# Turning the row maxima of an attention kernel on VectorE in 32 by 32 blocks, and its early maxima in pairs

## The reference, cut to what matters

```python
x = _layernorm(builder_state, g1, beta1)         # 4096 x 512
base_n = _layernorm(base_state, g1, beta1)       # 3202 x 512
q, k, v = (heads(q_in, Wq, bq), heads(kv_in, Wk, bk), heads(kv_in, Wv, bv))   # 8 heads of 64
scores = jnp.einsum('bhqd,bhkd->bhqk', q, k) * (1.0 / np.sqrt(HD))
attn = jax.nn.softmax(scores, axis=-1)
out = jnp.einsum('bhqk,bhkd->bhqd', attn, v)
x = residual + out @ W_o.T + b_o
...
```

## Time and profile before

| | us |
|---|---|
| median of 3 runs | 2254.17 (2253.38 to 2255.58) |
| the profiled execution | 2255.61 |
| its span | 2253.8 |
| PE busy | 2216.3 (98% of the span) |
| DVE busy | 1713.4 (76%) |
| POOL busy | 1584.2 (70%) |
| ACT busy | 1092.4 (48%) |
| weight loads of PE | 1279.2, beside its matmuls |

### The profile page before, as it was taken

How to read it: one execution, slowest core, us unless ns; L and a number is a source line. 1 busy time by engine, 2 the same in 40 slices (tenths; PEclk the granted TensorE clock), 3 DMA queues, 4 the chain that set the end, 5 groups by cost and what they waited for, 6 DMA issues and landing times.

```text
span 2253.8 us, 36015 instructions
## 1 busy us (share of the span) xinstructions
PE 2216.3 (98%) x14120; PEld 1279.2 (57%) x14120; DVE 1713.4 (76%) x2087; ACT 1092.4 (48%) x1418; POOL 1584.2 (70%) x1038
## 2 busy tenths in 40 slices
PE   8999999999999999999999999999999999999997
PEld 8998865555555555555555555555555555445774
DVE  7866546888888888888888888888888888763776
ACT  5654334444454444444544544444445444453454
POOL 1200027888888888888888888888888888889332
PEclk9999999999999999999999999999999999999999
DMA  7750226777777777777777777777777777787844
GB/s 273 233 162 10 75 85 139 156 157 160 156 159 160 159 170 168 171 170 167 168 161 160 167 170 171 171 171 164 163 163 165 167 166 166 160 182 159 265 149 150
DMA packets 170091, 365.45 MB, mean 162 GB/s; under 512 B 28537, under 2 KB 75001, under 8 KB 169410
## 3 DMA queue, kind: packets, MB, share of 16 engines
q0 software_dynamic: 59904, 218.13, 47.4%
q1 hardware_dynamic: 110018, 145.02, 20.3%
HBM read 95.82 MB, written 49.04 MB: 64 GB/s over the span
## 4 chain that ended last, share of the span: by engine, by line
PE 94%; DMA 1%; ACT 1%; DVE 1%; issue 1%; POOL 1%; SPq 0%; DVEq 0%; ACTq 0%; POOLq 0%
PE ps L1478 34%; PE ps L1343 11%; PE ps L1455 8%; PE ps L1457 8%; PE ps L1459 8%; PE ps L1447 5%; PE ps L1306 4%; PE ps L1314 3%; PE ps L1324 3%; PE ps L1545 3%; PE ps L1278 1%; DMA acca<-pt 1%; PE ps L1348 1%; PE ps L1488 1%; PE ps L1608 1%
## 5 line engine op out<-in xcount | busy, mean ns | idle before, releaser
L799 ACT ACTIVATE pt<-ps 128x1024 f32<-128x1024 f32 x800 | 777.6, 1021 | 891.8 <-PE ps L1459 882.0
L1005 DVE TENSOR_REDUCE mx_part<-ps 128x2 f32<-128x1024 f32 x768 | 938.1, 1221 | 339.5 <-PE ps L1343 339.5
L605 POOL TENSOR_TENSOR accp<-accp,pt 128x1024 f32<-128x1024 f32 x416 | 1032.9, 2483 | 210.0 <-ACT pt L799 204.7
L1478 PE MATMUL ps<-pt,v 128*64 128x512 f32 x3328 | 805.6, 605 | 0.0
L1094 DVE TENSOR_TENSOR ps<-ps,shb 128x1024 f32<-128x1024 f32 x403 | 493.2, 1224 | 46.7 <-PE ps L1459 46.7
L1478 PEld LDWEIGHTS ps<-pt,v 128*64 128x64 f32 x3328 | 201.8, 136 | 345.2 <-issue 339.0
L1343 PE MATMUL ps<-kk,qh 64*128 64x512 f32 x1520 | 344.4, 448 | 1.6 <-DVE mx_part L1005 1.6
L1343 PEld LDWEIGHTS ps<-kk,qh 64*128 64x128 f32 x1520 | 141.6, 183 | 340.9 <-DVE mx_part L1005 250.0
L1455 PE MATMUL ps<-qh,kk 64*128 64x512 f32 x1664 | 328.9, 390 | 2.7 <-ACT pt L799 2.7
L1457 PE MATMUL ps<-qh,kk 64*128 64x512 f32 x1664 | 329.3, 390 | 0.0
L1459 PE MATMUL ps<-ql,kk 64*128 64x512 f32 x1664 | 328.5, 389 | 0.0
(11 more groups left out here) (165 smaller groups left out, 1779.7 us busy)
## 6 DMA issues: line engine op xcount, KB each, us to landing
acca<-pt POOLq DMA_DIRECT2D x224, 512.0 KB, 4.9
accb<-pt POOLq DMA_DIRECT2D x160, 512.0 KB, 4.8
q_scratch<-kk SPq DMA_DIRECT2D x32, 512.0 KB, 4.3
acca<-accp POOLq DMA_DIRECT2D x32, 512.0 KB, 4.6
o_scratch<-ost SPq DMA_DIRECT2D x32, 512.0 KB, 3.1
og<-o_scratch SPq DMA_DIRECT2D x32, 512.0 KB, 6.2
shb<-m_scratch SPq DMA_DIRECT2D x31, 512.0 KB, 4.6
xs<-x SPq DMA_DIRECT2D x16, 512.0 KB, 6.5
```

Of the source, the lines that this page charges most:

```text
L605: nc.gpsimd.tensor_tensor(acc[:, :], acc[:, :], pt[n % PT_SLOTS][:, :], ALU.add).then_inc(added_p, 1)
L799: nc.scalar.activation(pt[n % PT_SLOTS][:, :], src, ACT.Exp, scale=SCALE).then_inc(exped, 1)
L1005: nc.vector.tensor_reduce(mx_part[w % 2][:, m % QT, :, m // QT], ps[:, b:b + 2, :], AX_X, ALU.max)\
L1478: ins = mm(ps[HD * h:HD * (h + 1), 6, :], v[:, t, f:f + HD], pt[n % PT_SLOTS][:, h * QB:(h + 1) * QB], start=(t == 0), stop=(t == NT - 1))
```

## The change

**Turning.** PE's `turn_max` and ACT's `shift` are gone. `mx_row` is now a tile of 32 columns, of which 8 are used. DVE turns it with one instruction behind the reduction, in four blocks of 32 by 32, into `mx_turn`: the 8 values of partitions 0 to 31 then lie in rows 0 to 7, those of partitions 32 to 63 in rows 32 to 39, and so on. SP sends them with four stores of 8 rows of 32 numbers, where it was one store of 8 rows of 128. The sign is changed no more: the row of ones is now one of -1, and DVE subtracts where it added. DVE waits for its own reduction before it turns, and for the stores of the unit before.

**Pairs.** In groups 2 to 11 of the context stage the second early maximum follows the first at once on PE. It goes to banks 0 and 1, which are free between `turn` of the next group and that of the one after it; the latter now waits for that maximum to be taken. DVE takes the first maximum behind the first low part of k, and the second behind the second one.

```diff
-        mx_row = at("mx_row", [P, 2, QT], RR + 11776)
+        mx_row = at("mx_row", [P, 32], RR + 11840, F32R)
+        mx_turn = at("mx_turn", [P, 32], RR + 11872, F32R)
...
 def max_bank(w, m):
+    if w == 0 and m % 2 == 1 and m < 2 * (C_G - 3):
+        return 0
     return 5 if (w, m) in EARLY else 4
...
             def send_shift(w):
-                sp.wait_ge(shift_ready, w + 1)
+                sp.wait_ge(max_ready, w + 1)
...
-                sp.dma_start(m_scratch[w % 2].rearrange("h (q k) -> (h q) k", k=P), shift_row[:, :].bitcast(F32)).then_inc(sh_stored, 16)
+                by_tile = m_scratch[w % 2].rearrange("h (q k) -> (h q) k", k=P)
+                for i in range(4):
+                    sp.dma_start(by_tile[:, 32 * i:32 * (i + 1)], mx_turn[32 * i:32 * i + 2 * QT, :].bitcast(F32)).then_inc(sh_stored, 16)
...
-            def shift(w):
-                act.wait_ge(max_turned, w + 1)
-                wait(act, sh_stored, 16 * w)
-                nc.scalar.activation(shift_row[:, :], ps[0:2 * QT, turn_bank(w), 0:P], ACT.Copy, scale=-1.0)\
-                    .then_inc(shift_ready, 1)
...
             def row_max(w):
...
-                nc.vector.tensor_reduce(mx_row[:, :, :].rearrange("p h q -> p q h"), mx_part[w % 2][:, :, :, :], AX_X, ALU.max)\
-                    .then_inc(max_ready, 1)
+                nc.vector.tensor_reduce(mx_row[:, 0:2 * QT].rearrange("p (h q) -> p q h", h=2), mx_part[w % 2][:, :, :, :], AX_X, ALU.max)\
+                    .then_inc(row_ready, 1)
+                dve.wait_ge(row_ready, w + 1)
+                wait(dve, sh_stored, 64 * w)
+                nc.vector.transpose(mx_turn[:, :].bitcast(F32), mx_row[:, :].bitcast(F32)).then_inc(max_ready, 1)
...
                     if n == 12:
                         dve.wait_ge(parts_loaded, 32)
+                        nc.vector.memset(mx_row[:, :].bitcast(F32), 0.0).then_inc(row_cleared, 1)
...
             def turn(n):
                 pe.wait_ge(normed, n + 1)
                 wait(pe, n_ready, 2 * n)
+                if second_max(n - 2 - X_G):
+                    pe.wait_ge(max_taken, nth_max(*second_max(n - 2 - X_G)) + 1)
...
             def maxima(w, m):
-                wait(pe, max_taken, nth_max(w, m))
+                if max_bank(w, m) == 0:
+                    wait(pe, max_taken, nth_max(w, m) - 1)
+                    pe.wait_ge(n_ready, 2 * (X_G + m // 2 + 2 + 2))
+                else:
+                    wait(pe, max_taken, nth_max(w, m))
...
-            def turn_max(w):
-
-                pe.wait_ge(max_ready, w + 1)
-                wait(pe, den_taken, w - 1)
-                if w == 0:
-                    pe.wait_ge(n_ready, 2 * NG)
-                nc.tensor.transpose(ps[0:2 * QT, turn_bank(w), 0:P], mx_row[:, :, :].rearrange("p h q -> p (h q)"), ident[:, :])\
-                    .then_inc(max_turned, 1)
...
-                        early_maxima(early[:1])
+                        early_maxima(early[:2])
                         project_v(n, 1)
-                        early_maxima(early[1:2])
```

More of the change, by code:

```diff
@@ L55, in maxima_of @@
     return [(i // NM, i % NM) for i in range(first, min(first + 2, NM * UNITS))]
-TURN_STEP = NJ - M_LEAD
 PAIR_ORDER = [2, 3, 0, 1]
@@ L133, in unit, with second_max @@
     return w % BLOCKS, PAIR_ORDER[w // BLOCKS]
+def second_max(g):
+    return (0, 2 * (g - 2) + 1) if 2 <= g < C_G - 1 else None
 def max_bank(w, m):
+    if w == 0 and m % 2 == 1 and m < 2 * (C_G - 3):
+        return 0
     return 5 if (w, m) in EARLY else 4
-def turn_bank(w):
-    return 7 if w else 0
 def k_slot(w):
@@ L236, in build @@
         ost = at("ost", [P, 2, QB], RR + 10240, F32R)
-        mx_row = at("mx_row", [P, 2, QT], RR + 11776)
+        mx_row = at("mx_row", [P, 32], RR + 11840, F32R)
+        mx_turn = at("mx_turn", [P, 32], RR + 11872, F32R)
         mx_part = [at("mx_part0", [P, QT, 2, 7], RR + 12032), at("mx_part1", [P, QT, 2, 7], RR + 11784)]
-        shift_row = at("shift_row", [2 * QT, P], RR + 11840, F32R)
         qx = at("qx", [P, QB], RR + 12096, F32R)
@@ L338, in build @@
         max_done = sem("max_done"); max_taken = sem("max_taken"); max_ready = sem("max_ready")
-        max_turned = sem("max_turned"); shift_ready = sem("shift_ready"); qx_loaded = sem("qx_loaded"); sh_loaded = sem("sh_loaded")
+        row_cleared = sem("row_cleared"); row_ready = sem("row_ready"); qx_loaded = sem("qx_loaded"); sh_loaded = sem("sh_loaded")
         scored = sem("scored"); sh_stored = sem("sh_stored"); shb_loaded = sem("shb_loaded")
@@ L409, in send_shift @@
             def send_shift(w):
-                sp.wait_ge(shift_ready, w + 1)
+                sp.wait_ge(max_ready, w + 1)
                 wait(sp, sh_loaded, 16 * (w - 1))
                 wait(sp, shb_loaded, 16 * (w - 2))
-                sp.dma_start(m_scratch[w % 2].rearrange("h (q k) -> (h q) k", k=P), shift_row[:, :].bitcast(F32)).then_inc(sh_stored, 16)
-                sp.wait_ge(sh_stored, 16 * (w + 1))
+                by_tile = m_scratch[w % 2].rearrange("h (q k) -> (h q) k", k=P)
+                for i in range(4):
+                    sp.dma_start(by_tile[:, 32 * i:32 * (i + 1)], mx_turn[32 * i:32 * i + 2 * QT, :].bitcast(F32)).then_inc(sh_stored, 16)
+                sp.wait_ge(sh_stored, 64 * (w + 1))
                 sp.dma_start(sh[w % 2][0:HD + 1:HD, :].bitcast(F32), m_scratch[w % 2]).then_inc(sh_loaded, 16)
@@ L576, in _ @@
             nc.gpsimd.memset(pad[0:KEYS - (NT - 1) * P, :], 0.0)
-            nc.gpsimd.memset(ones_row[0:1, :].bitcast(F32), 1.0)
-            nc.gpsimd.memset(ones_row[HD:HD + 1, :].bitcast(F32), 1.0).then_inc(ones_set, 1)
+            nc.gpsimd.memset(ones_row[0:1, :].bitcast(F32), -1.0)
+            nc.gpsimd.memset(ones_row[HD:HD + 1, :].bitcast(F32), -1.0).then_inc(ones_set, 1)
             pool.wait_ge(ones_set, 2)
@@ L770, in _ @@
                 high_k(C_G - 1, i)
-            shift(0)
             for t in range(GT):
@@ L825, in _ @@
                         high_o(u - 1)
-                    if j == TURN_STEP and u + 1 < UNITS:
-                        shift(u + 1)
                     if u == UNITS - 2 and j in (3, 5, 7, 9):
@@ L1000, in take_max @@
                 if m == 0:
-                    wait(dve, max_ready, w - 1)
+                    wait(dve, row_ready, w - 1)
                 dve.wait_ge(max_done, nth_max(w, m) + 1)
@@ L1013, in row_max @@
             def row_max(w):
+                if w == 0:
+                    dve.wait_ge(row_cleared, 1)
                 dve.wait_ge(max_taken, NM * (w + 1) if w else M_EARLY)
-                wait(dve, max_turned, w)
-                nc.vector.tensor_reduce(mx_row[:, :, :].rearrange("p h q -> p q h"), mx_part[w % 2][:, :, :, :], AX_X, ALU.max)\
-                    .then_inc(max_ready, 1)
+                nc.vector.tensor_reduce(mx_row[:, 0:2 * QT].rearrange("p (h q) -> p q h", h=2), mx_part[w % 2][:, :, :, :], AX_X, ALU.max)\
[3 more added lines that the diff above has]
+                nc.vector.transpose(mx_turn[:, :].bitcast(F32), mx_row[:, :].bitcast(F32)).then_inc(max_ready, 1)
             dve.wait_ge(cols_loaded, 16)
@@ L1071, in _ @@
                     if g < C_G - 1:
+                        low_k(g, 0)
                         for w, m in early[:1]:
                             take_max(w, m)
-                        for i in (0, 1):
-                            low_k(g, i)
+                        low_k(g, 1)
                         for w, m in early[1:2]:
@@ L1093, in add_shift @@
                 dve.wait_ge(scored, NT * u + t)
-                nc.vector.tensor_tensor(ps[:, b:b + 2, :], ps[:, b:b + 2, :], shb[u % 2][:, :, :], ALU.add)\
+                nc.vector.tensor_tensor(ps[:, b:b + 2, :], ps[:, b:b + 2, :], shb[u % 2][:, :, :], ALU.subtract)\
                     .then_inc(shifted, 1)
@@ L1425, in _ @@
             project_v(NG - 1, 0)
-            turn_max(0)
             project_v(NG - 1, 1)
             pe.wait_ge(k_ready, FC * C_G)
-            pe.wait_ge(shift_ready, 1)
+            pe.wait_ge(max_taken, M_EARLY)
             pe.wait_ge(ones_set, 2)
@@ L1484, in spread_sum @@
                 pe.wait_ge(added_a[u % 2], 16 * (len(A_TILES) + 1) * (u // 2 + 1))
-                if u + 1 < UNITS:
-                    pe.wait_ge(shift_ready, u + 2)
+                wait(pe, den_taken, u)
                 for i in range(4):
@@ L1521, in _ @@
                         score_tile(u, 2 * j + 1)
-                    if ahead and j == TURN_STEP:
-                        turn_max(u + 1)
                     for w, m in todo[1:]:
```

## The result

The changed kernel takes 2242.71 us (median of 5 runs, 2241.05 to 2245.54), the kernel before 2254.17 (5 runs, 2251.08 to 2256.29). The ratio is 0.9949, with a 95% interval from 0.9936 to 0.9962: 11.5 us, or 0.5%, faster. The forecast was 2237.6 with a range up to 2242.5. So the direction was right, the gain was 11.5 us where 16.6 were forecast, and the time lies 0.2 us above the range, which is less than the noise of these medians. The profiled execution took 2242.71 us as well, with a span of 2240.9; against that of before, 2255.61, it gained 12.9.

What follows compares the result with a forecast made beforehand. PE, busy 98% of the span, was taken to bound the kernel. Terms 12.5 + 4.1 + 0.3 - 0.3 = 16.6 us, off the median of 2254.17, gave 2237.6 us; range 2234.8 to 2242.5.

Steps and rivals of the forecast that it cites:

- what bounds the kernel: Whole kernel: PE is busy 98% of the span and makes 94% of the chain; the other engines wait for it.
- the mechanism: Step 9 of the units: removing the turning from PE saves 0.41 us in each of 30, 12.5 us in all.
- Unit 30: The only unit whose turned step has no maxima: 3.89 us against 3.69 for the next, so 0.20 us saved.
- whether PE can use it: Units: DVE's last maximum of step 9 holds PE's next step by 0.01 us a unit, 0.3 us lost.
- the pairs: Context stage: a second maximum directly behind the first saves 0.41 us in each of ten groups, 4.1 us.
- every stretch the change doesn't touch at nothing: Stretches outside the change, unit 31 among them: the sum had no term for them, 0 us.
- POOL: Rival, units: POOL can't keep up with the shortened step, 12.3 of 16.6 us return, time near 2250; chance 0.04.
- stores: Rival, units: the four stores land too late for the next unit's first shift matmul, time above 2260; chance 0.01.
- DVE: Rivals: DVE paces step 9 or pairs give little, 2239.7 to 2243.8, chance 0.10; slow turning, above 2260, chance 0.03.
- The clock: End of the context stage or elsewhere: the granted clock may fall or not, 1.6 us either way, only in the range.

Runs made afterwards that it cites:

- the padding: 32 tiny matmuls added in PE's idle time at the start: changed kernel 2237.75 us (0.9928 of before), kernel before 2258.86 us (1.0018).
- the changed kernel with 64 matmuls: The changed kernel with 64 tiny matmuls added where PE waits for the first weights: 2241.34 us, 0.9946 of before.
- the later loads: Output stage's first four loads (2 MB) issued behind unit 30's denominators: changed kernel 2238.16 us (0.9927), kernel before 2253.82 us (0.9997).
- the one wait: Changed kernel without DVE's repeated wait for its reduction before a unit's first maximum: 2239.08 us (0.9931); with 32 tiny matmuls too, 2239.06 us (0.9934).

## Why the prediction was wrong

**Right: what bounds the kernel, and the mechanism.** PE's row in the units was what counted. Taking the turning out of it shortened step 9 in all of them, and everything else of it (0.21 us on DVE, four stores) stayed hidden. Unit 30 was right too: its step 9, without maxima, fell from 3.89 us to 3.69. By their count the last maxima stand in step 8 of that unit and not in step 9; the term doesn't change by it.

**Mis-sized: whether PE can use it.** The prediction looked for DVE's hold at the next step's first maximum, and took 0.01 us a unit. PE was held by 0.03 to 0.04, at its second maximum of step 9 itself, which waits for DVE's first one. That one starts late by the doubled wait. The row was there: DVE at 411.17, 0.61 us behind PE's 410.56, with the turning still between it and PE's need. Priced: 12.2 us forecast, 11.3 measured. That the doubled wait is the cause rests on the profiles without it (step 9 at 4.15 us or less); no run's time shows it clear of noise.

**Mis-sized: the pairs.** 0.41 us each forecast, 0.37 measured, 0.4 us in all.

**Missing: the place of the code fetches.** The two mis-sized terms alone leave 15.3 of 16.6 us and a time inside the range. The step that failed is the one that put every stretch the change doesn't touch at nothing, unit 31 with them. The prediction lists waits of other kinds as rivals (POOL, stores, DVE), and none of those came. No step of it asked what else moves when PE has 32 turnings less to run: its code is shorter, so the fetches of code fall elsewhere against the program. In the changed kernel one meets a transfer for which PE has no time to spare, and costs 1.6 us in unit 31. The one that cost the kernel before 1.4 us in unit 29 is gone. That fetches move in this way is shown by the padding; what they come to in the whole time is less certain, since gains and losses of about 1.5 us stand at several places, and the clock fell for another 1.6 in unit 31.

Three comparisons bear on it, and none is clean. The changed kernel with the fetch moved away is at 0.9928 (0.9914 to 0.9941) of before, 16.4 us, but before has its own fetch in unit 29. With the fetch on this transfer in both, 2258.86 for before with the matmuls against 2242.71 and 2243.30, it is 15.6 to 16.2, over different chips. On one chip, against the changed kernel with 64 matmuls (2241.34), it is 17.5. All lie about the forecast of 16.6, and the intervals are some 3 us wide on either side.

**The clock** was taken as 1.6 us either way behind the last maxima of the context stage. It fell there in 7 of 13 profiles and not in the others, whatever the kernel, so that was rightly no term of the sum. The fall in unit 31, in 5 of the 13, was allowed for by "or elsewhere" and by the 1.6 us in the range, but not placed.

**Open:** what in the output stage takes back the gain of the later loads, when the clock falls in unit 31, why 32 matmuls together with the one wait bring no more than the matmuls alone, and the 0.7 us that the two places at the start differ by from execution to execution. Whether the 0.2 us above the range would be there again can't be told from these runs.

## What to carry to other kernels

When instructions are taken out of the engine that bounds a kernel, price the step by the distance between two starts with and without them, not by the length of their record: here 0.41 us against 0.27. Then look at every wait of that engine in the shortened step, not only the last one, since a wait that had 0.4 us to spare may now have none. And where a transfer is awaited with no time to spare, a change of the code's length alone can move a code fetch onto it, or away from it: an edit that does nothing but that (32 tiny matmuls in an idle place) tells such a loss from one of the change itself. Make it in the kernel before as well, since that one may have such a wait too.

## What the hardware showed

A fetch of 16 KB of code took 0.89 us, and the transfer of 512 KB that ran beside it in unit 31 landed after 6.0 to 6.3 us in eight profiles, instead of 4.4 in five without a fetch; one of its 16 parts came 1.7 us behind the others. The same padding of 32 matmuls moved the kernel before by +0.18% and the changed one by about -0.2%, as much as a whole small optimization; the fetch's wait is only a part of that.

A wait on a semaphore that was long fulfilled, in front of an instruction that has another wait, delayed DVE's start by 0.06 us.

A turning of 128 by 32 numbers in blocks took DVE 0.21 us, the same as a reduction of 128 by 56. Two maxima in a row in the context stage, between products of 128 rows, took 0.38 us less than the same two apart.
